# Keys' squares summed in two fp16 parts, image corrections in staggered halves, and the key and first-norm steps a slot later

## The reference

```
q = _l2norm(q) * scale * qn_g
k = _l2norm(k) * scale * kn_g
scores = jnp.einsum('bhqd,bhkd->bhqk', q, k) * dh ** (-0.5)
```

## Time and profile before

| what | value |
|---|---|
| median of 3 runs | 1461.5 us (1458.69 to 1461.71) |
| the profiled execution's own time | 1459.82 us |
| its span, first to last instruction | 1457.8 us |
| PE busy | 1415.5 us, 97% |
| DVE busy | 1215.5 us, 83% |
| ACT busy | 1106.4 us, 76% |
| POOL busy | 290.9 us, 20% |
| mean granted TensorE clock | 0.993 |
| chain that ended last | PE 74%, DVE 10%, DMA 7%, issue 5%, ACT 2% |

### The profile page before, as it was taken

How to read it: one execution, slowest core, us unless ns; L and a number is a source line. 1 busy time by engine, 2 the same in 40 slices (tenths; PEclk the granted TensorE clock), 3 DMA queues, 4 the chain that set the end, 5 groups by cost and what they waited for, 6 DMA issues and landing times.

```text
span 1457.8 us, 31164 instructions
## 1 busy us (share of the span) xinstructions
PE 1415.5 (97%) x10945; PEld 982.8 (67%) x10945; DVE 1215.5 (83%) x2576; ACT 1106.4 (76%) x1880; POOL 290.9 (20%) x293
## 2 busy tenths in 40 slices
PE   8998899999999999999999999999999999999997
PEld 5665667676676677676676677676676767676665
DVE  7886898888888888889788888889888888887765
ACT  5343678787878888887878878888878878878766
POOL 2124032131301212131301212131301112130101
PEclk9999999999999999999999999999999999999999
DMA  8796232434333332424233332424342332424334
GB/s 263 180 237 128 105 61 30 121 43 109 45 107 46 80 73 29 124 38 114 39 108 45 93 60 29 124 38 115 40 113 38 100 53 33 120 38 116 49 99 57
DMA packets 40771, 125.54 MB, mean 86 GB/s; under 512 B 5792, under 2 KB 6048, under 8 KB 38560
## 3 DMA queue, kind: packets, MB, share of 16 engines
q0 software_dynamic: 22464, 55.81, 26.3%
q1 hardware_dynamic: 18128, 69.28, 13.2%
q10 hardware_dynamic: 144, 0.01, 0.0%
HBM read 68.98 MB, written 50.48 MB: 82 GB/s over the span
## 4 chain that ended last, share of the span: by engine, by line
PE 74%; DVE 10%; DMA 7%; issue 5%; ACT 2%; DVEq 0%; POOL 0%; SPq 0%; POOLq 0%; ACTq 0%
PE pair L1094 25%; PE pair L1059 22%; PE pair L829 9%; PE pair L816 4%; DMA area<-gate_scratch 3%; DVE area L1537 3%; PE pair L1007 3%; PE pair L924 2%; PE pair L980 2%; PE pair L995 2%; DMA area<-area 2%; PE pair L955 1%; DVE area L1550 1%; DMA gate_scratch<-gt_t 1%; ACT area L672 1%
## 5 line engine op out<-in xcount | busy, mean ns | idle before, releaser
L667 ACT ACTIVATE area<-pair,pack_b_sb 128x680 f32<-128x680 f32 x512 | 423.5, 827 | 180.6 <-PE pair L1059 180.5
L1537 DVE TENSOR_TENSOR area<-area 128x680 f16<-128x680 f32 x512 | 454.0, 892 | 110.1 <-ACT area L672 104.1
L1059 PE MATMUL pair<-area,ws 128*128 128x340 f16 x3072 | 530.7, 308 | 5.5 <-ACT area L667 2.8
L1094 PE MATMUL pair<-area,ws 128*128 128x340 f16 x3072 | 526.8, 307 | 6.9 <-DVE area L1550 3.8
L1094 PEld LDWEIGHTS pair<-area,ws 128*128 128x128 f16 x3072 | 290.2, 98 | 160.6 <-DVE area L1550 26.4
L1059 PEld LDWEIGHTS pair<-area,ws 128*128 128x128 f16 x3072 | 292.4, 97 | 155.0 <-ACT area L667 8.3
L672 ACT ACTIVATE area<-pair,pack_b_sb 128x680 f16<-128x680 f32 x384 | 316.2, 824 | 0.0
L498 POOL DMA_DIRECT2D tower_out<-area x128 | 114.2, 892 | 997.3 <-DVE area L1550 943.4
L1550 DVE SCALAR_TENSOR_TENSOR area<-pair,pack_b_sb,area 128x340 f32<-128x340 f32 x256 | 133.9, 565 | 10.2 <-PE pair L1094 8.5
L633 ACT ACTIVATE area<-pair,nbias,root 85x85 f32<-85x85 f32 (+1 forms) x256 | 112.5, 466 | 0.2
L455 POOL TENSOR_TENSOR area<-area 128x680 f16<-128x680 f32 x56 | 89.2, 1601 | 45.3 <-ACT area L596 43.0
(11 more groups left out here) (238 smaller groups left out, 1758.5 us busy)
## 6 DMA issues: line engine op xcount, KB each, us to landing
tower_out<-area POOLq DMA_DIRECT2D x128, 340.0 KB, 4.7
area<-gate_scratch SPq DMA_DIRECT2D x16, 1360.0 KB, 9.9
area<-gate_scratch SPq DMA_DIRECT2D x16, 1020.0 KB, 7.1
area<-cells SPq DMA_DIRECT2D x16, 392.0 KB, 8.7
area<-cells POOLq DMA_DIRECT2D x14, 392.0 KB, 6.5
area<-area POOLq DMA_DIRECT2D x14, 392.0 KB, 6.3
tower_out<-ht SPq DMA_DIRECT2D x16, 340.0 KB, 2.3
area<-gate_scratch SPq DMA_DIRECT2D x16, 340.0 KB, 4.4
```

The costliest lines, as they stand in the source:

```text
L667: nc.scalar.activation(two(hid[slot % NHID]), halves(hid_ps[slot % 2]), ACT.Gelu_apprx_tanh, bias=col(COL_B1 + slot)).then_inc(hid_ready, 1)
L1059: last = mm(hid_ps[slot % 2][:, j, 0:TH], lhs[:, w], rhs[:, j * TH:(j + 1) * TH], start=(i == 0), stop=(i == 2))
L1094: last = mm(eo_ps[:, j, 0:TH], lhs[:, w], rhs[:, j * TH:(j + 1) * TH], start=(m % CH == 0 and i == 0), stop=(m % CH == CH - 1 and i == 2))
L1537: v.tensor_tensor(hl[slot % NPART], hid[slot % NHID], hh[slot % NPART], ALU.subtract).then_inc(hlo_ready, 1)
```

## The change

- The keys' squares are written twice by ScalarE, as fp16 and as fp32 (`sqk_h`, `sqk`); VectorE subtracts (new step `k_lo`); TensorE sums high and low parts against fp16 ones (`head_16`), 16 fp16 products in place of 8 fp32 ones. Group 0 keeps the old form.
- Each correction of an image is cut in two halves, `fixa` and `fixb`, of which the second comes a slot after the first.
- The tables move the key's steps (`sums_k` from slot 11 to 13, roots 11, 11, 12 to 13, 14, 14, `wide` 14 to 16, `cast` 16 to 18, `kn` 15 to 17) and the first norm's (one slot later; `root2`, `edges` and the ReLUs stay).
- In the start-up, the remaining row sums come three to four points later, after the last convolution; the folding of weights and `kn` of group 0 come earlier. The statistics of the 56 images are made within the first attention, and no longer in part in the first expert stage.

```diff
--- before.py
+++ after.py
@@ -60,10 +60,11 @@
 ACT_RELU = (0, 3)
 LN2_SLOTS = {"var2": 2, "roots2": 2, "cast": 5, "hx": 4, "hx_lo": 4}
 GATE_SLOTS = {"turn": 3, "turned": 1}
-QK_SLOTS = {"q": 7, "sums_q": 9, "k": 9, "sums_k": 11, "root0": 11, "root1": 11, "root2": 12, "wide": 14,
-            "cast": 16, "kn": 15}
-EARLY_SLOTS = {"fix0": 6, "fix1": 7, "fix2": 8, "fix3": 9, "tok_hi": 11, "mean": 18, "dev": 17, "sq": 19,
-               "sq_lo": 19, "var": 22, "root0": 22, "root1": 22, "root2": 23, "cast": 25, "xn": 24, "xn_lo": 25, "edges": 28,
+QK_SLOTS = {"q": 7, "sums_q": 9, "k": 9, "k_lo": 11, "sums_k": 13, "root0": 13, "root1": 14, "root2": 14, "wide": 16,
+            "cast": 18, "kn": 17}
+EARLY_SLOTS = {"fixa0": 6, "fixb0": 7, "fixa1": 7, "fixb1": 8, "fixa2": 8, "fixb2": 9, "fixa3": 9,
+               "fixb3": 10, "tok_hi": 11, "mean": 19, "dev": 18, "sq": 20,
+               "sq_lo": 20, "var": 23, "root0": 23, "root1": 23, "root2": 23, "cast": 26, "xn": 25, "xn_lo": 26, "edges": 28,
                "relu0": 28, "relu1": 29, "relu2": 30, "relu3": 31}
 SUMS_AT = T // 2
 
@@ -73,7 +74,7 @@
 GRAPH_0 = {"plain": 24, 0: 24, 1: 24, 2: 24, 3: 24, "h2": 29, "mean2": 27, "dev2": 32, "sq2": 26, "var2": 30,
            "roots2": 37, "cast": 35, "hx": 38, "hx_lo": 39}
 QK_0 = {"q": 41, "sums_q": 44, "k": 47, "sums_k": 51, "root0": 58, "root1": 59, "root2": 60, "wide": 58,
-        "cast": 62, "kn": 73}
+        "cast": 62, "kn": 65}
 FIRST_1 = {"fix0": 29, "fix1": 30, "fix2": 39, "fix3": 46, "mean": 44, "dev": 49, "sq": 45, "var": 46,
            "root0": 52, "root1": 52, "root2": 53, "cast": 50, "xn": 57, "xn_lo": 58, "edges": 54, "relu0": 51,
            "relu1": 52, "relu2": 55, "relu3": 55}
@@ -88,13 +89,12 @@
 ALONE = 4
 PE_PREP = {4: 2, 13: 3, 14: 4, 22: 5}
 DVE_PREP = {1: 1, 4: 2, 14: 3, 22: 5, 23: 6, 24: 7, 25: 8, 35: 9}
-DVE_SUMS = {62: 0, 63: 1, 64: 2}
+DVE_SUMS = {66: 0, 67: 1, 68: 2}
 ACT_PREP = {1: 3, 13: 4, 15: 5, 25: 6}
 ACT_SQUARES = {4: 2, 7: 3, 14: 4, 25: 5, 26: 6, 28: 7, 37: 8, 41: 9, 43: 10, 45: 11, 48: 12, 49: 13}
-IMG_SLOT = 4
 FOLD_PE = {0: 27, 1: 30, 2: 35, 3: 41, 4: 59, 5: 59, 6: 68, 7: 69}
 FOLD_HI = {0: 26, 1: 31, 2: 37, 3: 41, 4: 56, 5: 60, 6: 70, 7: 73}
-FOLD_LO = {0: 36, 1: 36, 2: 42, 3: 46, 4: 64, 5: 69, 6: 77, 7: 77}
+FOLD_LO = {0: 36, 1: 36, 2: 42, 3: 46, 4: 64, 5: 65, 6: 69, 7: 70}
 W2_ROW = 10
 ONE_HOT = (10, 0, 3, 3)
 MASKED = -1e30
@@ -160,6 +160,7 @@
         mean_16 = sb("mean_16", [128, 128], F16)
         count_m = sb("count_m", [128, 128])
         head_m = sb("head_m", [128, 128])
+        head_16 = sb("head_16", [128, H], F16)
         mask = sb("mask", [QC, QC], mybir.dt.bfloat16)
         identb = sb("identb", [QC, QC], mybir.dt.bfloat16)
         conv_u = sb("conv_u", [128, NP * NP])
@@ -224,6 +225,7 @@
         dev, sq, h1 = take(T), take(T), take(4 * T)
         h1_h, h1_l = (h1[:, 2 * n * T:2 * (n + 1) * T].bitcast(F16) for n in range(2))
         sqk, fix = h1[:, 0:T], h1[:, T:T + NB * NP * NP]
+        sqk_h, sqk_l = (h1[:, 2 * T:3 * T].bitcast(F16)[:, k * T:(k + 1) * T] for k in range(2))
         xh, qs, kb, sqq = (take(T) for _ in range(4))
         relu = (xh, sqq, dev, sq)
         xh_h, xh_l = take(T // 2).bitcast(F16), take(T // 2).bitcast(F16)
@@ -284,7 +286,7 @@
         mean2_ps, dev2_ready, sq2_ready, var2_ps = map(sem, ("mean2_ps", "dev2_ready", "sq2_ready", "var2_ps"))
         hx_ready, hxh_ready, hxl_ready, split_step = map(sem, ("hx_ready", "hxh_ready", "hxl_ready", "split_step"))
         q_ps, q_ready, k_ps, k_ready = map(sem, ("q_ps", "q_ready", "k_ps", "k_ready"))
-        ss_ready, ss_ps, wide_ready, kn_ready = map(sem, ("ss_ready", "ss_ps", "wide_ready", "kn_ready"))
+        ss_ready, sl_ready, ss_ps, wide_ready, kn_ready = map(sem, ("ss_ready", "sl_ready", "ss_ps", "wide_ready", "kn_ready"))
         vp_ps, vp_ready, score_ps, max_ready = map(sem, ("vp_ps", "vp_ready", "score_ps", "max_ready"))
         nb_ready, exp_ready, rs_ready, p_ready = map(sem, ("nb_ready", "exp_ready", "rs_ready", "p_ready"))
         pt_ps, pt_ready, pv_ps = map(sem, ("pt_ps", "pt_ready", "pv_ps"))
@@ -438,7 +440,8 @@
             pool.memset(mean_16[:, :], 1.0 / D).then_inc(pool_prep, 1)
             pool.wait_ge(pool_prep, 15)
             pool.tensor_copy(ident16[:, :], ident[:, :]).then_inc(pool_prep, 1)
-            pool.wait_ge(pool_prep, 16)
+            pool.tensor_copy(head_16[:, :], head_m[:, 0:DH + 1:DH]).then_inc(pool_prep, 1)
+            pool.wait_ge(pool_prep, 17)
             pool.tensor_copy(identb[:, :], ident[0:QC, 0:QC]).then_inc(consts_ready, 1)
 
 
@@ -605,7 +608,7 @@
 
                     var_evac(g, "ln2", var2_ps, TILES, 1.0 + EPS_LN, 2)
 
-            def queries_keys(g, step):
+            def queries_keys(g, step, later=True):
                 if step == "q":
                     act.wait_ge(q_ps, g + 1)
                     nc.scalar.activation(two(sqq), halves(fr_ps), ACT.Square, bias=att_b[:, 0:1]).then_inc(ss_ready, 1)
@@ -613,6 +616,8 @@
                                          scale=gq[:, 1:2]).then_inc(q_ready, 1)
                 if step == "k":
                     act.wait_ge(k_ps, g + 1)
+                    if later:
+                        nc.scalar.activation(two(sqk_h), halves(fr_ps), ACT.Square, bias=att_b[:, 1:2])
                     nc.scalar.activation(two(sqk), halves(fr_ps), ACT.Square, bias=att_b[:, 1:2]).then_inc(ss_ready, 1)
                     nc.scalar.activation(two(kb), halves(fr_ps), ACT.Identity, bias=att_b[:, 1:2]).then_inc(k_ready, 1)
                 if step == "sums_k":
@@ -693,7 +698,7 @@
                 for step in steps_in(GRAPH_0, n):
                     graph(0, step)
                 for step in steps_in(QK_0, n):
-                    queries_keys(0, step)
+                    queries_keys(0, step, later=False)
                 for step in steps_in(FIRST_1, n):
                     early(1, step, later=False, ps=hid_ps[1])
                 for e in steps_in(FOLD_HI, n):
@@ -934,10 +939,18 @@
                     sums(0, sqq)
                 if step == "k":
                     of_hx(D).then_inc(k_ps, 1)
-                if step == "sums_k":
+                if step == "sums_k" and not later:
                     pe.wait_ge(k_ready, g + 1)
                     pe.wait_ge(ss_ready, 2 * (g + 1))
                     sums(1, sqk).then_inc(ss_ps, 1)
+                if step == "sums_k" and later:
+                    pe.wait_ge(k_ready, g + 1)
+                    pe.wait_ge(sl_ready, g)
+                    for t in range(TILES):
+                        c, tile = SUMS_AT + 2 * (TILES + t), slice(t * QC, (t + 1) * QC)
+                        mm(fr_ps[0:QC, 0, c:c + 2], sqk_h[:, tile], head_16[:, :], start=True, stop=False)
+                        last = mm(fr_ps[0:QC, 0, c:c + 2], sqk_l[:, tile], head_16[:, :], start=False, stop=True)
+                    last.then_inc(ss_ps, 1)
                 if step == "cast":
                     cast_roots(g, "qk")
 
@@ -947,8 +960,8 @@
                     pe.wait_ge(half_ready, g * E)
                 if b == 2 and later:
                     pe.wait_ge(tmp_ready, g * E)
-                if b == 0 and not later:
-                    pe.wait_ge(tok_done, 2 * NP)
+                if b == 2 and not later:
+                    pe.wait_ge(img_step[1], 3)
                 for k in range(2):
                     t = 2 * b + k
                     for n, (x_part, w_part) in enumerate(((xh_h, wv_h), (xh_l, wv_h), (xh_h, wv_l))):
@@ -970,7 +983,7 @@
                 if later:
                     hidden_read(g - 1, SLOTS - 2 + m)
                 elif m == 1:
-                    pe.wait_ge(img_step[1], 3)
+                    pe.wait_ge(fold_lo, E)
                 for b in (2 * m, 2 * m + 1):
                     ps = score_ps_at(b)
                     for c in range(2):
@@ -1022,6 +1035,8 @@
                 if not later:
                     for m in range(NB // 2):
                         scores(g, m, later)
+                    pe.wait_ge(tok_done, 2 * NP)
+                    image_stats(1, BZ, eo_ps[:, 1, 0:2 * BZ])
                 graph_of("plain", 0)
                 for b in range(NB):
                     values(g, b, later)
@@ -1142,8 +1157,6 @@
                     prepare(PE_PREP[n])
             for n in LATE:
                 chain(n)
-            pe.wait_ge(fold_lo, E)
-            image_stats(1, BZ, hid_ps[1][:, 1, 0:2 * BZ])
             pe.wait_ge(tok_done, 2 * NP - 2)
             attention(0, False, True)
             with pe.Fori(1, G - 1) as g:
@@ -1366,13 +1379,15 @@
 
             def early(g, step, ps=fr_ps):
                 if step[:3] == "fix":
-                    b = int(step[3])
+                    b = int(step[-1])
                     fix_b, h_b = fix[:, b * NP * NP:(b + 1) * NP * NP], ht[:, bass.ds(g * T + (b * TOK + 1), NP * NP)]
```

(26 more changed lines are left out.)

## The result

| what | before | after |
|---|---|---|
| median of the runs | 1461.6 us (1458.69 to 1463.63, 4 runs) | 1506.2 us (1502.49 to 1507.7, 4 runs) |
| ratio, with its 95% interval | 1 | 1.0299 (1.0282 to 1.0316) |
| span of the profiled execution | 1457.8 us | 1503.9 us |
| its own time | 1459.82 us | 1505.75 us |

What follows compares the result with a forecast made beforehand. TensorE, busy 80.91 of each 81.75 us period, was taken to set the end. Fourteen full stages (+35.3), +1 in the first, -0.5 keys-only and -6.4 start-up gave +29.4, so 1491 us, range 1464 to 1500 (forecast's own 1480 to 1499).

Steps and rivals of the forecast that it cites:

- keys' sums, TensorE: Sixteen fp16 products replace the fp32 sums on TensorE: 0.65 us for 1.16, -0.51 per stage, bounds 0.3 to 0.6 saved.
- wait for the keys' subtraction: Before the keys' sums, TensorE waits while GpSimd's token subtraction holds VectorE's: +1.66 us per stage, bounds 0 to 2.
- mean waits for the scaled keys: Key scaling moves two slots, the mean one, so TensorE waits at the mean: +0.15 us per stage, bounds 0 to 0.6.
- squares in slot 20, bank of slot 23: First norm's squares on ScalarE delay slot 21's fp16 copy, so TensorE waits for slot 23's bank: +0.25 us, bounds 0 to 0.5.
- end of the first norm: Low part comes behind VectorE's weighing, copy and subtraction in slot 26, delaying edge products: +0.97 us per stage, bounds 0.3 to 1.2.
- full stage without a fall: Sum of the five per-stage terms for a full expert stage: +2.52 us, by 14 +35.3.
- first stage, without its fall: First expert stage: a full stage's cost plus +1 us, as GpSimd also splits weights on the same stretch.
- start-up: Earlier normalisation (about 3.0 us) and image factors out of the first expert stage (3.4): -6.4 us, bounds -4 to -8.
- first rival: Keys' subtraction slips in before GpSimd's: wait 0.35 us, a stage +1.21, in all +10.0, 1471 us; chance 0.17.
- faster: Staggered corrections put VectorE ahead of TensorE everywhere, no wait at either low part: -14.1 us, 1447; chance 0.14.
- only the norm's end waits: Only the first norm's end makes TensorE wait: +0.46 us by 14, in all -0.5, 1461 us; chance 0.07.
- no cheaper: The fp16 sums of the keys cost TensorE as much as fp32: 15 by 0.51 us above forecast, 1499; chance 0.06.

Runs made afterwards that it cites:

- experiment 5: Kernel before, with only the end of the first norm (turn of roots, multiplication, low part) a slot later: 1477.4 us, ratio 1.0104.
- experiment 1: Kernel after, with ScalarE's fp16 copy of the tokens in slot 12 instead of 11: 1478.9 us, ratio 1.011 to the kernel before.
- experiment 6: Experiment 1's kernel with the first norm's steps from the variance on back in their old slots, mean and squares still late: 1468.1 us, ratio 1.0039.
- Experiment 3: Kernel after, with 24 products nobody reads put on TensorE ahead of its wait for the keys' subtraction: 1496.3 us, ratio 1.0235.
- experiment 4: Kernel before, with only the start-up part of the change, all slots as before: 1455.3 us over 6 runs, ratio 0.9952.
- experiment 7: Kernel after, with the keys' subtraction in slot 10, sums in 12, later key steps one slot earlier, first norm in its old slots: 1470.8 us, ratio 1.0054.
- experiment 9: Experiment 7's kernel with the second and third root step of the keys in slot 14, behind an expert's weighing: 1475.7 us, ratio 1.0101.
- experiment 2: Kernel after, with the keys' sums back in fp32 in slot 13, without the second square and `k_lo`: 1473.3 us, ratio 1.0076.

## Why the prediction was right in sign and wrong in size

The time, 1506.2, lies above the range (1464 to 1500) and 15 above the 1491. Held against the forecast by its own steps, in the profiled execution, where +29.4 was forecast and +46.1 came:

| step | forecast | measured |
|---|---|---|
| keys' sums, TensorE | -0.51 | 0.65 for 1.16: -0.51 |
| wait for the keys' subtraction | +1.66 | +1.70 |
| mean waits for the scaled keys | +0.15 | +0.14 |
| squares in slot 20, bank of slot 23 | +0.25 | +0.22 |
| end of the first norm | +0.97 | +1.05 (alone, experiment 5) |
| full stage without a fall | +2.52 | 2.57 (33.5 over 13) |
| fall of the clock behind the wait | no term | 1.67, 8 times: +13.4 |
| first stage, without its fall | +3.5 | +2.8 |
| keys-only stage and the end | -0.5 | -0.3 |
| start-up | -6.4 | -3.2 in the trace: +2.2 ahead of the change, -5.4 in it |

The norm's +1.05 is also what its two waits in the trace of the kernel after give: 0.45 and 0.87, less 0.27 that the weighing had cost at this place before. The five rows add to 2.60, and the period's 2.57 agree.

**The waits** came out where and as large as worked out. GpSimd's hold of the keys' subtraction, which the first rival denied, stands by experiment 1; the norm's end by experiments 5 and 6. The forecast counted the turn of the roots to the edge products as 5.35; it is 5.43. The rivals all fall: *slips in before GpSimd* would have shown the 0.86 us that only experiment 1 has; *faster* and *only the norm's end waits* would have shown no wait on `k_lo`; *no cheaper* is contradicted by the 0.65.

**The step that failed** is the sum of a stage: it took each wait at its own length and assumed that TensorE goes on behind it at the clock of the period, 1.00. The rows for doubt were there: the earlier trace rows show a projection at 1.32 in place of 0.75 behind an idle stretch of 3.00, and the prediction even booked 0.57 for it in the start-up. It did not ask the same of the wait of 1.66 that the change puts into 14 stages. With the fall in every one of them the sum would have been 23 higher, with none nothing; in fact it came in 8, 13.4 us, four fifths of the 16.7 that the trace lies above the forecast. The upper bound of the range should have taken the full 23 in. Experiment 3 shows the cause, by the same wait without the idle. (The lower bound was wrong too: it took the start-up's bound of 8 off a sum that already had the 6.4. By its own terms it was 1470. This decided nothing.)

**The start-up** looks like a second miss, 3.2 us in place of 6.4, and is hardly one. The trace of the kernel after is already 2.2 late at group 0's query projection, where the change has done nothing yet that TensorE needs; its first products wait 7.8 us for their data, for 6.4 before. Counted from there, VectorE normalises 3.6 earlier (148.86, for 150.25), where 3.0 was forecast, and the first query projection of the expert stages comes 5.4 earlier, where the forecast had 5.8 (3.0 and 2.84). The 3.00 wait there is gone, as forecast. Alone, the part measures 5.0 in this stretch of its trace, and 6.8 by the medians, with bounds of 5 and 9 (experiment 4).

**The first stage** was booked at +1 for GpSimd's weight splits on top of the wait. The wait on `k_lo` is indeed longest there, 3.0 idle against 1.54 in a steady stage, so the booked 1 was 1.5; the mean's wait of 0.65 is longer too. But the stage without its fall is only 2.8 longer than before, not 3.5, since it had lost time before that it no longer loses:

```profile
177.53:180.20 2.67, 2.67 (x10) 1.48 (x11) 2.67 (x5) 0.75 (x2) 0.69 (x1) 0.50 0.95 400
```

```profile
197.87 1.08 PE L1094 MATMUL pair<-area,ws 128*128 128x340 f16 x6 [0.96 <-DVE area L1550]
```

In the kernel before, TensorE ran 2.67 us at the lower clock behind the 3.00 wait, which is 1.3 lost. The prediction had booked 0.57 of it, for the first four products alone. And it was idle for 0.96 before a half that VectorE was still weighing. Neither stands in the trace of the kernel after.

What stays open: why the clock fell behind 8 of 14 waits that look alike in the rows. The traces show the stretches, not what decides. Nor does the length of one wait decide by itself: in the first stages of experiments 7, 4 and 9 TensorE was idle once for 1.5, 1.9 and 2.1 us without a fall. No run sets such waits into every stage, so how often they would bring one is not shown.

## What to carry to other kernels

A wait put into the queue of the engine that sets the end costs its length and, where TensorE's granted clock falls behind it, here about as much again: look for an idle stretch of that length elsewhere in the same trace and read the steps behind it, and give the range both. Before a step is moved by a slot, list what every engine owes in the slot it moves to; experiments 5 and 7 lost some 15 us each, one because a moved step came behind a weighing and a subtraction, the other because moved steps came ahead of a weighing, on an engine with 12 us to spare in the period. And a cheaper form on one engine (0.51 us saved on TensorE) can cost latency on the others. Here one more operation on VectorE ahead of the sums ate it: at best 0.07 us of a steady stage was left (83.06 in experiment 1, 83.13 with the old sums in experiment 2), and the first stage was 3.9 longer, its fall of the clock included.
